# Packing the attention scores as two 64-row tiles, splitting the maxima on GpSimd, and turning them two ticks later

## The reference

```python
def ffn(x):                      # per batch element: 512 tokens, 128 channels, 16 heads of 8
    x = conv3(x) + conv_b                                   # 3 taps, 128 x 128
    q, k, v = split(x @ wqkv.T + bqkv)
    scores = einsum('bhqd,bhkd->bhqk', q, k) / sqrt(8)      # 16 heads, 512 x 512 each
    ctx = einsum('bhqk,bhkd->bhqd', softmax(scores), v)
    x = layernorm(x + ctx @ wo.T + bo, ln1_g, ln1_b)
    probs = softmax(x @ gate_w + gate_b)                    # 8 experts, all of them computed
    h = relu(einsum('bsd,edf->bsef', x, w1) + b1)           # 128 -> 512, per expert
    y = einsum('bsef,efd->bsed', h, w2) + b2                # 512 -> 128
    return layernorm(x + einsum('bse,bsed->bsd', probs, y), ln2_g, ln2_b)

x = x + 0.5 * ffn(norm(x))
x = x + dilated_attention(norm(x))                          # small: 16 steps per segment and offset
x = x + 0.5 * ffn(norm(x))
```

## Time and profile before

| | us |
|---|---|
| median of 3 runs | 1826.52 (1823.33 to 1830.15) |
| the profiled execution, its own time | 1823.7 |
| its span | 1822.0 |
| PE busy | 1713.5 (94%) |
| DVE busy | 1397.8 (77%) |
| ACT busy | 1083.7 (59%) |
| POOL busy | 1005.6 (55%) |

### The profile page before, as it was taken

How to read it: one execution, slowest core, us unless ns; L and a number is a source line. 1 busy time by engine, 2 the same in 40 slices (tenths; PEclk the granted TensorE clock), 3 DMA queues, 4 the chain that set the end, 5 groups by cost and what they waited for, 6 DMA issues and landing times.

```text
span 1822.0 us, 29053 instructions
## 1 busy us (share of the span) xinstructions
PE 1713.5 (94%) x8605; PEld 960.8 (53%) x8752; DVE 1397.8 (77%) x2855; ACT 1083.7 (59%) x1964; POOL 1005.6 (55%) x829
## 2 busy tenths in 40 slices
PE   4789999999999999999999999999999999999976
PEld 2224555555555555555555555555555555555555
DVE  4777777777777878788787787888878777767687
ACT  2566666666666656566665666656656566665633
POOL 5412556665755656465565655656556565655232
PEclk7899999999999999999999999999999999999988
DMA  4211112121212212122121211212122121210111
GB/s 138 87 39 55 52 28 77 33 69 32 77 42 59 62 36 73 43 68 59 37 82 28 82 48 39 77 36 79 42 64 62 37 68 30 77 36 31 36 39 25
DMA packets 89773, 99.46 MB, mean 55 GB/s; under 512 B 14928, under 2 KB 65920, under 8 KB 89600
## 3 DMA queue, kind: packets, MB, share of 16 engines
q1 hardware_dynamic: 88336, 93.40, 18.1%
q0 software_dynamic: 1280, 4.20, 0.8%
HBM read 77.63 MB, written 20.19 MB: 54 GB/s over the span
## 4 chain that ended last, share of the span: by engine, by line
PE 77%; DVE 13%; issue 4%; DMA 2%; ACT 2%; POOL 1%; SPq 1%; DVEq 0%; ACTq 0%; POOLq 0%
PE ctx_ps L1038 12%; PE score1a L1025 6%; PE hid_ps L910 6%; PE hid_ps L914 6%; PE y_ps L910 6%; PE y_ps L914 5%; PE score1b L1025 5%; PE y_ps L911 5%; PE hid_ps L911 5%; PE score2b L1018 5%; DVE negmax L751 4%; PE score2a L1018 4%; DVE hidh L721 2%; PE misc L976 1%; PE misc L910 1%
## 5 line engine op out<-in xcount | busy, mean ns | idle before, releaser
L497 POOL TENSOR_TENSOR hidl<-hid,hidh 128x512 fp32r<-128x512 f32 x456 | 590.4, 1295 | 559.7 <-DVE hidh L721 542.8
L620 ACT ACTIVATE hid<-hid_ps,cols 128x512 f32<-128x512 f32 x484 | 333.0, 688 | 377.8 <-PE hid_ps L914 359.4
L751 DVE TENSOR_REDUCE negmax<-score1a 128x1 f32<-128x512 f32 x512 | 351.2, 686 | 201.6 <-PE score1a L1025 196.5
L596 ACT ACTIVATE probs<-score2a 128x512 f32<-128x512 f32 x512 | 305.0, 596 | 138.9 <-PE score2a L1018 78.3
L751 DVE TENSOR_REDUCE negmax<-score1b 128x1 f32<-128x512 f32 x512 | 349.5, 683 | 35.1 <-PE score1b L1025 33.6
L596 ACT ACTIVATE probs<-score2b 128x512 f32<-128x512 f32 x512 | 303.5, 593 | 35.7 <-PE score2b L1018 35.6
L1038 PE MATMUL ctx_ps<-probs,V 128*9 128x512 f32 x2048 | 268.6, 596 | 1.2
L721 DVE CAST hidh<-hid 128x512 fp32r<-128x512 f32 x512 | 252.0, 492 | 12.5 <-ACT hid L620 12.5
L910 PE MATMUL hid_ps<-x1h,w1h 128*128 128x512 f32 x484 | 258.3, 534 | 2.8 <-ACT x1h L605 2.7
L1025 PE MATMUL score1a<-Kp,Qp 96*128 96x512 bf16 x512 | 198.5, 388 | 39.5 <-DVE negmax L751 19.9
L910 PE MATMUL y_ps<-hidh,w2h 128*128 128x512 f32 x512 | 210.9, 412 | 7.8 <-DVE gated L732 7.4
(11 more groups left out here) (185 smaller groups left out, 2255.1 us busy)
## 6 DMA issues: line engine op xcount, KB each, us to landing
gate_b<-gate_dram SPq DMA_DIRECT2D x128, 256.0 KB, 3.7
q_parts_dram<-q_parts SPq DMA_DIRECT2D x48, 128.0 KB, 2.3
k_parts_dram<-k_parts SPq DMA_DIRECT2D x48, 128.0 KB, 2.3
Qp<-q_parts_dram SPq DMA_DIRECT2D x64, 96.0 KB
Kp<-k_parts_dram SPq DMA_DIRECT2D x64, 96.0 KB
gate_b<-in_L_ffn_w POOLq DMA_DIRECT2D x16, 256.0 KB, 3.6
Qp<-q_parts_dram SPq DMA_DIRECT2D x64, 64.0 KB
Kp<-k_parts_dram SPq DMA_DIRECT2D x64, 64.0 KB
```

The source lines that it names most:

```text
L497: pool.tensor_tensor(hidl[:, n % RING, :], hid[:, n % 2, :], hidh[:, n % RING, :].bitcast(F32), ALU.subtract).then_inc(s["h_lo"], 1)
L596: act.activation(probs[:, n % 2, j, :], score2[(T - P2_AT) % 2][:], ACT.Exp, scale=SCALE)\
L620: act.activation(hid[:, n % 2, :], hid_bank(u, n)[:], ACT.Relu, bias=col(n))\
L751: dve.tensor_reduce(negmax[:, g % 2, T % 16:T % 16 + 1], score1[T % 2][:], AX.X, ALU.max, negate=True).then_inc(s["a_max"], 1)
```

## The change

- **Pairs.** Heads i and i+8 are computed together. `Qp` and `Kp` hold eight pairs: head i on partitions 0 to 47, head i+8 on partitions 64 to 111. Each score matmul contracts over 48 rows (51 in the second pass) in place of 96 (128), and stands in a tile of 64 rows. The two of a pair write two different banks. All ticks of the scores become even ticks with two matmuls each; one reduce and one exponential of 1024 columns read both banks.
- **Banks.** `score1` and `score2` are now one pair of banks each: the matmuls of a pair wait until the reduce (the exponential) of the pair before has ended. Before, they waited for the one before the last.
- **Maxima.** GpSimd splits the maxima before they are turned: four small steps on 128 x 16, written at T = 17 + 16g. TensorE then turns all 48 columns in one bf16 matmul at T = 19 + 16g, ScalarE copies them out in one step, and SP writes them with two transfers at T = 20 + 16g.
- **Loads.** `Qp` and `Kp` exist twice, by the parity of the unit, and are filled in two chunks (pairs 0 and 1, then 2 to 7) in place of four groups. A load of K no longer waits for the load of Q before it. The set-up writes ones into 32 rows of each half of `Kp`, and no zeros.

```diff
-        score1 = [psum("score1a"), psum("score1b")]
-        score2 = [psum("score2a"), psum("score2b")]
+        score1 = ctx.enter_context(nc.psum_tensor("score1", [128, 2, 512], F32))
+        score2 = ctx.enter_context(nc.psum_tensor("score2", [128, 2, 512], F32))
...
-        NM_AT = {17 + 16 * g: g for g in range(G)}
+        NM_AT = {19 + 16 * g: g for g in range(G)}
...
-        LOADS_AT = ({-19: 0, -6: 1, 9: 2, 25: 3}, {-16: 0, -6: 1, 9: 2, 25: 3})
+        LOADS_AT = {-19: (0, 0), -16: (1, 0), -7: (0, 1), -5: (1, 1)}
...
 # GpSimd
+                if T + 2 in NM_AT:
+                    g = NM_AT[T + 2]
+                    top, mid_part, low = (nm_parts[:, :, part, :] for part in range(3))
+                    wait(pool, s["a_max"], u.count(32, 8 * g + 8))
+                    wait(pool, s["a_nmT"], u.count(4, g))
+                    pool.tensor_copy(top, negmax[:, g % 2, :, :]).then_inc(s["a_n1"], 1)
+                    wait(pool, s["a_n1"], u.count(4, g + 1))
+                    pool.tensor_tensor(nm_rest[:], negmax[:, g % 2, :, :], top, ALU.subtract).then_inc(s["a_nr"], 1)
+                    wait(pool, s["a_nr"], u.count(4, g + 1))
+                    pool.tensor_copy(mid_part, nm_rest[:]).then_inc(s["a_n2"], 1)
+                    wait(pool, s["a_n2"], u.count(4, g + 1))
+                    pool.tensor_tensor(low, nm_rest[:], mid_part, ALU.subtract).then_inc(s["a_n3"], 1)
...
 # ScalarE
-                    act.activation(m_parts[:, 0, :], misc[0:HG * TC, 0:128], ACT.Copy).then_inc(s["a_m1"], 1)
-                if T - 1 in NM_AT:
-                    g = NM_AT[T - 1]
-                    wait(act, s["a_r1"], u.count(4, g + 1))
-                    act.activation(m_parts[:, 1, :], m_rest[:], ACT.Copy).then_inc(s["a_m2"], 1)
+                    act.activation(m_rows[:], misc[0:3 * HG * TC, 0:128], ACT.Copy).then_inc(s["a_mr"], 1)
...
 # VectorE
-                if 0 <= T < 64:
-                    wait(dve, s["a_s1"], u.count(64, T + 1))
-                    dve.tensor_reduce(negmax[:, g % 2, T % 16:T % 16 + 1], score1[T % 2][:], AX.X, ALU.max,
+                if 0 <= T < 64 and T % 2 == 0:
+                    k = T // 2
+                    wait(dve, s["a_s1"], u.count(32, k + 1))
+                    dve.tensor_reduce(negmax[:, g % 2, :, k % 8], score1[:], AX.X, ALU.max,
                                       negate=True).then_inc(s["a_max"], 1)
...
 # TensorE
-                    wait(pe, s["a_max"], u.count(64, 16 * g + 16))
-                    pe.transpose(misc[0:HG * TC, 0:128], negmax[:, g % 2, :], ident[:]).then_inc(s["a_nmT"], 1)
+                    wait(pe, s["a_n3"], u.count(4, g + 1))
+                    pe.matmul(misc[0:3 * HG * TC, 0:128], nm_parts[:].rearrange("p t a k -> p (t a k)"), ident_b[:],
+                              start=True, stop=True).then_inc(s["a_nmT"], 1)
...
-                    wait(pe, s["a_exp"], u.count(64, k - 1))
-                    pe.matmul(score2[k % 2][:], Kp[:, g * HG + j, kc * 128:(kc + 1) * 128],
-                              Qp[:, g * HG + j, :], start=True, stop=True).then_inc(s["a_s2"], 1)
+                    wait(pe, s["a_exp"], u.count(32, k))
+                    for half in range(2):
+                        rows = slice(HALF * half, HALF * half + ALL_ROWS)
+                        last = pe.matmul(score2[:, half, :], Kp[p][rows, 2 * g + j, kc * 128:(kc + 1) * 128],
+                                         Qp[p][rows, 2 * g + j, :], start=True, stop=True)
+                    last.then_inc(s["a_s2"], 1)
...
-                    wait(pe, s["a_max"], u.count(64, T - 1))
-                    pe.matmul(score1[T % 2][:], Qp[0:SCORE_ROWS, h, qc * 128:(qc + 1) * 128],
-                              Kp[0:SCORE_ROWS, h, :], start=True, stop=True).then_inc(s["a_s1"], 1)
+                    wait(pe, s["a_max"], u.count(32, k))
+                    for half in range(2):
+                        rows = slice(HALF * half, HALF * half + SCORE_ROWS)
+                        last = pe.matmul(score1[:, half, :], Qp[p][rows, pair, qc * 128:(qc + 1) * 128],
+                                         Kp[p][rows, pair, :], start=True, stop=True)
+                    last.then_inc(s["a_s1"], 1)
```

More of the change, by code:

```diff
@@ L197, in chunks @@
             return tile[:].rearrange("p (c d) -> p c d", c=TC)
+        s["pack_in"] = [sem(f"pack_in{k}") for k in range(len(LOAD_CHUNKS))]
         s["parts_out"] = [sem("q_parts_out"), sem("k_parts_out")]
@@ L270, in hid_bank @@
         def hid_bank(u, n):
-            return score1[0] if alone(u, n) and n % 2 else hid_ps
+            return score1[:, 0, :] if alone(u, n) and n % 2 else hid_ps[:]
         def wait_lo(eng, u, k):
@@ L344, in tick @@
                                 .then_inc(s["parts_out"][k], 16)
-                for k, (Tk, g) in [(k, at) for k in range(2) for at in LOADS_AT[k].items()]:
-                    if T != Tk:
-                        continue
+                if T in LOADS_AT:
+                    k, chunk = LOADS_AT[T]
+                    lo, hi = LOAD_CHUNKS[chunk]
                     wait_sp(s["parts_out"][k], u.count(48, 48))
[L350 to L367, removed]
+                    wait_sp(s["a_s2"], (u.n - 1) * 32)
+                    wait_sp(s["pack_ones"], 4)
@@ new lines, in tick @@
+                    for half in range(2):
+                        for row, n, part, step in RUNS_OF_PARTS[k]:
+                            src = dram[k][part:part + (n if step else 1), :,
+                                          PAIRS * half + lo:PAIRS * half + hi, :]\
+                                .rearrange("a d i q -> a d (i q)")
+                            if not step:
+                                src = src.to_broadcast([n, DH, (hi - lo) * S])
+                            at = HALF * half + row * DH
+                            sp.dma_start((Qp, Kp)[k][u.parity][at:at + n * DH, lo:hi, :]
+                                         .rearrange("p i q -> p (i q)"), src).then_inc(s["pack_in"][chunk], 16)
@@ L1037, in tick @@
                     for j in range(HG):
-                        last = pe.matmul(ctx_ps[32 * j:32 * j + DH + 1, :], V[p][:, kc, g * HG + j, :],
-                                         probs[:, n % 2, j, :], start=(kc == 0), stop=(kc == TC - 1))
+                        half, pair = divmod(j, 2)
+                        last = pe.matmul(ctx_ps[32 * j:32 * j + DH + 1, :], V[p][:, kc, PAIRS * half + 2 * g + pair, :],
+                                         probs[:, n % 2, 2 * pair + half, :], start=(kc == 0), stop=(kc == TC - 1))
                     last.then_inc(s["a_pv"], 1)
```

139 lines of the change are left out of this document (77 added, 62 removed).

## The result

| | before | after |
|---|---|---|
| median | 1824.92 us (1822.71 to 1830.15, 4 runs) | 1861.66 us (1857.23 to 1863.04, 4 runs) |
| ratio | | 1.0193, 95% interval 1.0164 to 1.0222 |
| span of the profiled execution | 1822.0 | 1860.5 |
| PE busy | 1713.5 (94%) | 1631.2 (88%) |

The kernel is 37 us slower, where I forecast 15. TensorE is busy for 82 us less and idle for 121 us more.

What follows compares the result with a forecast made beforehand. TensorE's queue was taken as the bound, busy for 96.7 of 100 us. The terms -225 + 126 + 120 + 4 - 10 = +15 gave 1839 on the profiled execution, 1842 on the median, stated as 1840; range 1738 to 1940.

Steps and rivals of the forecast that it cites:

- the term for the loads: Loads of Q and K in the head, where first scores wait for K: 0, within 10 us either way.
- part 3: Turn of the maxima: TensorE waits for GpSimd's split of 2.4 us, +120 us; ScalarE's copies in middle blocks, +4.
- part 4: Single banks, long reduce and bursts, partly hidden in other waits: -10 us, with -40 and +60 as ends.
- Parts 1 and 2: Score matmuls on TensorE: the two of a pair run together, -225 us; changes of array shape cost +126 us.
- The 0.26 for each of the 48 added changes: Array shape changes: lost overlap of 0.16 and a load of 0.10 us each would put the sum 77 us higher.
- a pair saves 35%: Score pairs on TensorE: an estimate of 35% saved, not 50% of 451 us, putting the sum 68 us higher.
- the split is cheap: Rival at the turn of the maxima: GpSimd's steps at a memset's price, waits of 28 us, time 1750; chance 0.24.
- 64 waits that I had named: Sign at TensorE's turns: waits for GpSimd's parts, 64 times, some 2 us each, longest at t = 3 and 19.
- The sign that I had named for single banks: First-pass waits for `negmax` below 3 us a unit; the rival, bursts holding up pairs, said 1888 us, chance 0.16.

Runs made afterwards that it cites:

- the early split: The changed kernel with GpSimd's four steps on the maxima written one tick earlier, at T = 16 + 16g, ahead of `hidl`: 1841.04 us.
- the half reduce: The changed kernel with loads in four chunks, GpSimd's split one tick earlier, and VectorE's reduce over 256 of each bank's 512 columns: 1726.89 us.
- both mends and the early fetch: The changed kernel with loads in four chunks, GpSimd's split one tick earlier, and the middle block's input fetched at T = -8: 1782.72 us.
- four chunks: The changed kernel with `Qp` and `Kp` loaded in four chunks of two pairs in place of two chunks: 1813.14 us.

## Why the prediction was wrong

The direction was right and the size was not: +37, with +15 forecast. The step that failed is the term for the loads, put at 0 within 10: it measured 48.5 us. Two more terms were mis-sized, the split (in part 3) and the long reduce (in part 4), and their errors partly cancel. Taken in the order of the experiments, each against the one before, the difference is

| | us |
|---|---|
| changed kernel | 1861.66 |
| big chunk ahead of the middle block's input | -48.5 |
| split behind `hidl` | -30.2 |
| reduce of 1024 columns: banks and VectorE's load | -56.0 |
| what is left (with half of the reduce left out) | 1726.89, that is 98 below before |

The shares depend on the order: the early split alone takes 20.6 us off the changed kernel, since the late fetch hides it in the middle iterations.

- **Parts 1 and 2, held.** -225 + 126 = -99 was forecast. The 98 that are left above are a remainder and no measurement of these two parts alone. TensorE's busy time is one: in an iteration without the middle block it is 102.5 us before, 96.3 in the changed kernel and 96.2 with the half reduce, each at a granted clock of 1.00, so 6.2 less; forecast were 64 x 0.22 - 7.7 = 6.4. The pitch of a pair (0.23) and the entry (0.09) are as forecast. Out to the experts it is 0.31 - 0.22 + 0.34 - 0.23 = 0.20 against 0.23. Over the whole run PE's busy time fell by 82 where I said some 100, its share to the 88% named; the clock lost behind the late fetch is in the 82, and with both mends and the early fetch, at a mean clock near that of before (0.984 and 0.981), it is 100 less (1613.7). The Trainium skill (TensorEngine Tiling (Array Packing), Key Properties) has a change of mode drain TensorE; the rows show that a change costs 0.09 to 0.10, and 0.20 over two starts out to the experts, but not whether the array drains. The 0.26 for each of the 48 added changes (overlap and load) is not borne out. The Trainium skill's 3.07x for four row tiles (TensorE: Matmul & The Clock Gate, Measured speedup vs the span model) led to an estimate that a pair saves 35%; the timeline shows 48%, 0.23 for two in place of 0.44.
- **Part 3, failed in a term.** The sum for GpSimd's readiness took the split at 2.4 us, from subtractions at 0.72 and copies at 0.5. They measured 0.22 to 0.24 and 0.20, about a third of the 128 x 4 addition and 0.3 from start to start. The waits came to 29.6 us in place of 120, and the premise of the rival "the split is cheap" (28 us) is what happened. It gave no faster kernel. The rest of the sum was right where the waits are: at t = 3 TensorE comes after 3.5 us and `hidl` ends after 3.4. Of the 64 waits that I had named, 30 are there.
- **Part 4, too small.** -10 was taken for single banks and bursts, with +60 as the far end; the half reduce puts the cost at up to 56, near that end. The sign that I had named for single banks, waits of the first pass for `negmax` below 3 us a unit, fails in the changed kernel (77.5 / 16 = 4.8) and holds with the fetch in time (43.9 / 16 = 2.7). What I left out is that not only the banks wait for a long reduce: `ctxs`, `x1l` and `hidh` stand behind it, and the experts behind them. How the 56 divide among banks, small steps and VectorE's load stays open; no run here has the full reduce with two pairs of banks.
- **The loads, the step that failed.** For the loads I looked only at the head, and took 0 within 10. That the chunk of six pairs is issued at T = -7 and -5, which is t = 57 and 59 of the iteration before, and so ahead of the middle block's fetch in SP's order, was there to be read in the change. Twelve loads with 1.15 MB now stand in front of one transfer for which VectorE waits in order. Before, six loads with 384 KB stood there (2 x (96 + 64 + 32) KB); with four chunks twelve loads with 384 KB do no harm, so it is not their number. That is 48.5 us, more than the whole slowdown.

In numbers: +1 for parts 1 and 2, -94 for the turn (124 with its middle-block share, against 30), +66 for the reduce (56 against -10), +48 for the loads: +21 in all. That the forecast lay no further off, and that the direction came out, is luck: large errors of both signs cancel.

## What to carry to other kernels

When transfers are merged or moved, list what now stands behind them in the same queue, and ask for each who waits for it in order; a fetch whose data have long been ready should be issued ahead of a burst. When two short operations become one long one, the total may fall and the small steps behind it still come late: look at the longest occupation in front of each short, urgent step. And when a sum lands near zero, its terms need their own check, since large ones of both signs can hide behind a right total.

## What the runs showed of the hardware

The landing of a fetch behind a burst depends on more than the busy share of the DMA engines while it waits. Behind twelve loads with 384 KB it lands after 3.1 us, behind twelve with 1.15 MB after 10.8. The busy time in three stretches of the changed kernel, the DMA share the last but one column:

```profile
938.00:940.00 2.00, 2.00 (x17) 1.18 (x10) 1.97 (x6) 0.77 (x1) 1.83 (x3) 1.00 0.94 346
944.00:950.00 6.00, 4.95 (x28) 2.33 (x24) 4.32 (x7) 3.00 (x4) 5.92 (x5) 1.00 0.91 183
952.00:957.50 5.50, 4.08 (x19) 2.14 (x18) 0.43 (x2) 3.04 (x5) 2.06 (x5) 1.00 0.15 53
```

After 952 only 0.15 x 16, some 2.4 engines' worth, is busy, and yet the fetch lands at 958.3. A plausible reading is that the loads pile up unevenly, and every transfer ends with the fullest of its engines; no run here tests it. Four small steps of GpSimd on 128 x 16 are 0.20 to 0.24 us each in most cases, about 0.3 from start to start when each waits for the last, while a power on 128 x 4 takes 1.04.
